# Turning the attention probabilities on VectorE in 32x32 blocks in the third stage of a decoder kernel

## The reference

```python
qkv = x @ Wqkv                       # x: 64 x 128, 16 heads of 64
q, k = rotary(l2norm(q) * qs), rotary(l2norm(k) * ksc)
sim = q @ k.T * 8                    # per head, 64 x 64
mask = (i < j) | (i > j + 32)        # causal, and at most 32 tokens back
attn = softmax(where(mask, -inf, sim))
y = y + concat_heads(attn @ v) @ Wo
y = y + (a * gelu(gate)) @ W2 + b2   # a, gate = split(layernorm(shift(y)) @ W1 + b1)
```

## Time and profile before

| what | value |
|---|---|
| time, median of 3 runs | 3386.17 us (3384.32 to 3388.98) |
| span of the profiled execution | 3389.4 us |
| PE busy in the span | 3317.7 us (98%) |
| DVE, ACT, POOL busy | 2767.5 (82%), 2803.2 (83%), 2483.0 us (73%) |
| share of PE in the chain that ended last | 95% |
| the third stage | about 565 us to the end |

### The profile page before, as it was taken

How to read it: one execution, slowest core, us unless ns; L and a number is a source line. 1 busy time by engine, 2 the same in 40 slices (tenths; PEclk the granted TensorE clock), 3 DMA queues, 4 the chain that set the end, 5 groups by cost and what they waited for, 6 DMA issues and landing times.

```text
span 3389.4 us, 120739 instructions
## 1 busy us (share of the span) xinstructions
PE 3317.7 (98%) x49605; PEld 2474.5 (73%) x49605; DVE 2767.5 (82%) x5297; ACT 2803.2 (83%) x5522; POOL 2483.0 (73%) x4812
## 2 busy tenths in 40 slices
PE   8989998999999999999999999999999999999997
PEld 6777876577777777777777777777777777777776
DVE  6844445888888888888888888888888888899995
ACT  5756665688888888888888888888888888888885
POOL 4622223888888888888888888888888888888884
PEclk8999999999999999999999999999999999999999
DMA  3000001544444444445444444444444444444441
GB/s 108 3 7 9 8 9 35 102 83 84 85 91 98 94 84 82 83 94 105 88 82 83 89 94 98 85 86 83 95 102 83 85 85 92 83 89 85 89 88 41
DMA packets 200381, 260.15 MB, mean 77 GB/s; under 512 B 123161, under 2 KB 145438, under 8 KB 199838
## 3 DMA queue, kind: packets, MB, share of 16 engines
q0 software_dynamic: 55296, 201.35, 31.4%
q1 hardware_dynamic: 143820, 50.88, 6.1%
q10 hardware_dynamic: 722, 0.21, 0.0%
HBM read 23.95 MB, written 2.10 MB: 8 GB/s over the span
## 4 chain that ended last, share of the span: by engine, by line
PE 95%; DVE 2%; POOL 1%; issue 1%; DMA 1%; ACT 1%; SPq 0%; DVEq 0%; POOLq 0%
PE bank L1059 19%; PE bank L1034 17%; PE bank L1110 10%; PE bank L1187 10%; PE bank L1158 8%; PE bank L1174 6%; PE bank L1129 5%; PE bank L1051 4%; PE bank L675 2%; PE bank L1124 2%; PE bank L688 2%; PE bank L697 2%; PE bank L752 2%; PE bank L367 1%; PE bank L660 1%; PE bank L377 1%
## 5 line engine op out<-in xcount | busy, mean ns | idle before, releaser
L1348 DVE TENSOR_TENSOR R<-bank,tables 128x1024 f32<-128x1024 f32 x768 | 904.7, 1220 | 174.7 <-ACT sq L1246 167.2
L1059 PE MATMUL bank<-WA,xcT 128*128 128x512 f32 x1536 | 723.6, 593 | 3.0 <-ACT xcT L1221 2.1
L1034 PEld LDWEIGHTS bank<-ident,R 128*128 128x128 f32 x3072 | 365.0, 141 | 214.7 <-issue 201.2
L1361 DVE TENSOR_REDUCE ss<-sq 128x16 f32<-128x1024 f32 x384 | 460.1, 1198 | 0.0
L1473 POOL TENSOR_TENSOR P<-P,inv_sum 128x512 f32<-128x512 f32 x384 | 447.6, 1331 | 2.9 <-DVE inv_sum L1402 2.9
L1246 ACT ACTIVATE sq<-bank 128x512 f32<-128x512 f32 x768 | 431.3, 587 | 16.0 <-PE bank L1059 16.0
L1034 PE MATMUL bank<-ident,R 128*128 128x128 f32 x3072 | 431.2, 273 | 8.8 <-POOL R L1461 6.8
L1461 POOL TENSOR_TENSOR R<-R,rn 128x512 f32<-128x512 f32 x384 | 400.4, 1043 | 31.5 <-DMA R<-R 5.4
L1467 POOL TENSOR_TENSOR P<-P,rn 128x512 f32<-128x512 f32 x384 | 402.6, 1048 | 4.3 <-DVE P L1390 4.3
L1059 PEld LDWEIGHTS bank<-WA,xcT 128*128 128x128 f32 x1536 | 262.2, 191 | 188.9 <-issue 184.0
L1187 PE MATMUL bank<-WO,OT 128*128 128x128 f32 x3072 | 374.6, 275 | 0.0
(11 more groups left out here) (154 smaller groups left out, 6857.6 us busy)
## 6 DMA issues: line engine op xcount, KB each, us to landing
R<-R POOLq DMA_DIRECT2D x384, 512.0 KB, 5.0
WA<-in_wqkv SPq DMA_DIRECT2D x24, 256.0 KB, 2.9
ystat<-Y SPq DMA_DIRECT2D x192, 32.0 KB
ystat<-Y SPq DMA_DIRECT2D x384, 15.8 KB
ys<-Y SPq DMA_DIRECT2D x192, 32.0 KB
ys<-Y SPq DMA_DIRECT2D x384, 15.8 KB
WV<-in_wqkv SPq DMA_DIRECT2D x6, 512.0 KB, 4.0
WO<-in_wo SPq DMA_DIRECT2D x6, 512.0 KB, 4.3
```

What stands on the lines that cost most here:

```text
L1034: return nc.tensor.transpose(dst, src, m.ident[:, :])
L1059: mm(b[QK_BANK[n, half]][:, :], m.xsT[:, t % 2, :], cols[:, half, :, :], start=True, stop=True)\
L1348: tt(both, src.unsqueeze(1).to_broadcast([128, 2, 16, 32]), tab.unsqueeze(2).to_broadcast([128, 2, 16, 32]), ALU.mult).then_inc(s.rotated. ...
L1361: nc.vector.tensor_reduce(m.ss[:, t % 2, 16 * n:16 * n + 16], m.sq[:, n, :].rearrange("p (h d) -> p h d", d=HD), AX.X, ALU.add)\
```

## The change

In the third stage, TensorE no longer turns the probabilities and ScalarE no longer copies them out of PSUM. Instead:

- VectorE turns each half of a tile's P (128x512) with one instruction of 32x32 blocks, into a new buffer Z (two tiles of it). Z has three slots of 256 columns for each head parity; the blocks of keys 0 to 31 go to slot 1, those of keys 32 to 63 to slot 2. These two instructions stand between `squares_summed(i, KEYS)` and `ff_added(i-8)`, and the first also waits until TensorE has read Z for the tile before last.
- A block turned in place lies in the partitions of its queries. SyncE therefore moves two blocks for each sequence with DMAs (four a tile, each 32 partitions by two runs of 1 KB): slot 1 of the first 32 partitions to slot 0, and slot 1 of the second 32 to slot 2 of the first 32. What the masked block leaves is zero; slot 0 of the second 32 partitions is zeroed once by GpSimd, in front of its cross-attention loop. The four DMAs stand at the end of SyncE's pass, behind `weights(i)`, and wait for VectorE.
- `head_outputs` reads Z in slots 0 and 2 (a moving operand of 2 x 32 columns), 32 products of 64x64 as before, and waits for the DMAs.
- `values` makes two products of full width (128 rows by 512 columns), where there were four with 64 output rows each, so V lies by token and not by sequence. The copies into V stay two of 512 columns.
- The copies of the head outputs (OT) write in another column order, and `out_projection` reads eight adjacent pieces.
- Waits follow: `input_turned` on `o_copied` in place of `p_copied`, `queries(t, 1)` on `v_copied`; `less_maximum` no longer waits for TensorE's turning.

The core of the diff:

```diff
+        m.Z = sb("Z", [128, 2, 2, 3, 256])
...
+        pool.memset(m.Z[:, :, :, :, :], 0.0)
         for i in range(N + 2):
             probs_scaled(i - 1, 1)
...
+        def probs_moved(t):
+            if exists(t):
+                sp.wait_ge(s.p_turned.sem, s.p_turned.upto(0, t + 1))
+                z, done = m.Z[:, t % 2, :, :, :], s.p_moved[t % 2]
+                for bb in range(2):
+                    first, second = slice(64 * bb, 64 * bb + 32), slice(64 * bb + 32, 64 * bb + 64)
+                    sp.dma_start(z[first, :, 0, :], z[first, :, 1, :]).then_inc(done, 16)
+                    sp.dma_start(z[first, :, 2, :], z[second, :, 1, :]).then_inc(done, 16)
...
             if i < N:
                 weights(i)
+            probs_moved(i - 3)
...
-                for e in range(2):
-                    last = mm(V_BANK[bb][64 * e:64 * e + 64, :], m.xsT[:, t % 2, bb * 64:bb * 64 + 64],
-                              cols[:, e, :, :], start=True, stop=True)
-                last.then_inc(s.v.sem, 1)
+                mm(V_BANK[j][:, :], m.xsT[:, t % 2, :], m.WV[:, j * 512:(j + 1) * 512], start=True, stop=True)\
+                    .then_inc(s.v.sem, 1)
...
-        def probs_turned(t, j):
-            if exists(t):
-                pe.wait_ge(s.normal.sem, s.normal.upto(j, t + 1))
...
-                for n in range(4):
-                    at = j * 512 + n * 128
-                    last = turned(PT_BANK[j][:, n * 128:(n + 1) * 128], m.P[:, t % 2, at:at + 128])
-                last.then_inc(s.p_turned.sem, 1)
...
+                for hp in range(PAIRS):
+                    for bb, a in ((0, 0), (1, 1), (0, 1), (1, 0)):
+                        rows, head, vals = slice(64 * bb, 64 * bb + 64), slice(64 * a, 64 * a + 64), (2 * hp + a) * 64
+                        probs = m.Z[rows, t % 2, a, 0:3:2, hp * 32:hp * 32 + 32]
+                        last = mm(PV_BANK[bb][head, hp * 64:hp * 64 + 64], m.V[rows, t % 4, vals:vals + 64], probs,
+                                  start=True, stop=True)
...
-        def probs_out(t, j):
-            if exists(t):
-                act.wait_ge(s.p_turned.sem, s.p_turned.upto(j, t + 1))
-                copy(m.PT[:, t % 2, j * 512:(j + 1) * 512], PT_BANK[j][:, :]).then_inc(s.p_copied.sem, 1)
...
+        def probs_turned(t, a):
+            if exists(t):
+                dve.wait_ge(s.normal.sem, s.normal.upto(a, t + 1))
+                if a == 1:
+                    at_least(dve, s.o, 2 * (t - 1))
+                blocks = m.P[:, t % 2, a * 512:(a + 1) * 512].rearrange("p (h k n) -> p k h n", k=2, n=32)
+                nc.vector.transpose(m.Z[:, t % 2, a, 1:3, :].rearrange("p k (h n) -> p k h n", n=32), blocks)\
+                    .then_inc(s.p_turned.sem, 1)
...
             squares_summed(i, KEYS)
+            probs_turned(i - 3, 1)
+            probs_turned(i - 3, 0)
             ff_added(i - 8)
```

More of the change, by code:

```diff
@@ L1066, in queries @@
                     pe.wait_ge(m.w_in, 64 * layer(t) + 64)
+                else:
+                    at_least(pe, s.v_copied.sem, s.v_copied.upto(1, t))
                 heads_in(t, QUERIES, half)
@@ L1097, in queries_turned, with values @@
                 last.then_inc(s.q_turned.sem, 1)
-        def values(t, bb):
+        def values(t, j):
             if exists(t):
-                cols = m.WV[:, :].rearrange("p (j e n) -> p e j n", e=2, n=128)
-                if bb == 1:
+                if j == 1:
                     pe.wait_ge(m.w_v, 16 * layer(t) + 16)
@@ L1132, in scores @@
                             last.then_inc(s.scores, 1)
-        def probs_turned(t, j):
-            if exists(t):
-                pe.wait_ge(s.normal.sem, s.normal.upto(j, t + 1))
-                if j == 0:
-                    at_least(pe, s.o_copied.sem, s.o_copied.upto(1, t))
-                else:
-                    pe.wait_ge(s.v_copied.sem, s.v_copied.upto(1, min(t + 4, N)))
-                    if t >= N - 3:
-                        pe.wait_ge(s.xn_copied, t - 2)
-                for n in range(4):
-                    at = j * 512 + n * 128
-                    last = turned(PT_BANK[j][:, n * 128:(n + 1) * 128], m.P[:, t % 2, at:at + 128])
-                last.then_inc(s.p_turned.sem, 1)
         def ff_in(t):
@@ L1163, in head_outputs @@
             if exists(t):
-                pe.wait_ge(s.p_copied.sem, s.p_copied.upto(0, t + 1))
+                pe.wait_ge(s.p_moved[t % 2], 64 * (t // 2) + 64)
                 pe.wait_ge(s.v_copied.sem, s.v_copied.upto(0, t + 1))
@@ L1168, in head_outputs @@
                     pe.wait_ge(s.rotated.sem, s.rotated.upto((QUERIES, 0), t + 5))
-                for j in range(4):
-                    for bb in range(2):
-                        for e, a in ((0, 0), (1, 1), (0, 1), (1, 0)):
-                            keys, head = slice(64 * e, 64 * e + 64), slice(64 * a, 64 * a + 64)
-                            vals, probs = bb * 512 + j * 128 + a * 64, (4 * a + j) * 128 + bb * 64
-                            last = mm(PV_BANK[e][head, j * 128 + bb * 64:j * 128 + bb * 64 + 64],
-                                      m.V[keys, t % 4, vals:vals + 64], m.PT[keys, t % 2, probs:probs + 64],
-                                      start=True, stop=True)
-                            if j == 3 and bb == 1 and (e, a) in ((0, 1), (1, 0)):
-                                last.then_inc(s.o, 1)
+                for hp in range(PAIRS):
[4 more added lines that the diff above has]
+                                  start=True, stop=True)
+                        if hp == PAIRS - 1 and (bb, a) in ((0, 1), (1, 0)):
+                            last.then_inc(s.o, 1)
         def out_projection(t):
@@ L1185, in out_projection @@
                 for c in range(PAIRS):
-                    at = (c % 2) * 512 + c // 2 * 128
-                    last = mm(OUT[:, 0:128], m.OT[:, t % 2, at:at + 128], wo[:, c * 128:(c + 1) * 128],
+                    last = mm(OUT[:, 0:128], m.OT[:, t % 2, c * 128:c * 128 + 128], wo[:, c * 128:(c + 1) * 128],
                               start=(c == 0), stop=(c == PAIRS - 1))
@@ L1230, in outputs_out @@
                 act.wait_ge(s.o, 2 * t + 2)
-                copy(m.OT[:, t % 2, e * 512:(e + 1) * 512], PV_BANK[e][:, :]).then_inc(s.o_copied.sem, 1)
+                copy(m.OT[:, t % 2, :].rearrange("p (c b q) -> p b c q", b=2, q=SEQ)[:, e, :, :],
+                     PV_BANK[e][:, :].rearrange("p (c q) -> p c q", q=SEQ)).then_inc(s.o_copied.sem, 1)
         def normal_out(t):
```

12 lines of the change are left out of this document (3 added, 9 removed).

## The result

| | before | after |
|---|---|---|
| median of the runs | 3387.43 us (3384.32 to 3388.98) | 3599.82 us (3596.59 to 3608.22) |
| profiled span | 3389.4 us | 3601.1 us |
| one pass of the third stage, median | 14.45 us | 15.46 us |

The changed kernel takes 1.0633 times as long, 95% interval 1.0617 to 1.0649. The forecast was 3576 us, 5.6% slower; it came out 6.3% slower, inside the range of 3465 to 3680 us.

The account below looks back on a forecast made before the run. TensorE, busy 98% of the span, was taken as the bound; afterwards a round through ff_added of 15.48 us replaces 14.45. 184 passes add 190 us: span 3579, time 3576 us, 5.6% slower, range 3465 to 3680.

Parts of the forecast that it names:

- The round through `ff_added`: From ff_in over TensorE, ScalarE and VectorE's ff_added back to ff_in: 15.48 us a pass after the change.
- The turnings: Two new VectorE instructions of 128x512 float32 in front of ff_added: 0.60 us each, 1.20 us a pass.
- The quick and the slow rival: VectorE's turnings at 0.32 us each, 3472 us, chance 0.07; or at 1.14 us each, 3774 us, chance 0.07.
- The gain on TensorE: Turnings of P and part of the values leave TensorE: 1.08 us a pass, all becoming idle time.
- the values: TensorE's products into V, two full ones for eight half-width instructions: 1.72 us instead of 1.87, 0.15 less.
- 3.9 us against 2.02 of issues: SyncE's queue behind the moves: time left for ys before the statistics need them, against their three issues; no wait counted.
- The rival for late ys: ys reach the statistics 1 us late through SyncE's queue or DMA: 0.64 us a pass, about 3694 us; chance 0.07.
- step 4: The two new turnings on VectorE, in front of ff_added, as part of the round: 1.20 us.
- the rival *Faster: VectorE's work bounds the pass at 13.98 us, 3300 us; needs turnings under 0.17 us together on the round; chance 0.04.
- The clock: TensorE's granted clock falls to its lower level in the longer wait: 2.3 us a pass, near 4000 us; chance 0.03.
- The prediction's own sign of being wrong: In the third stage, a granted clock below 1.00 would show the forecast wrong.
- What would show it: Third stage: passes of about 15.5 us, ff_in waiting 1.8 to 2.1 us for VectorE, turnings near 0.68 us.

Follow-up runs that it names:

- experiment 1: The kernel before with two VectorE turnings of a 128x512 buffer nobody reads, in front of ff_added in each pass: 3571.67 us, ratio 1.0542.
- experiment 5: The changed kernel with SyncE's DMAs of ystat issued one pass earlier, in front of the moves, all moves kept: 3571.4 us, ratio 1.0547.
- experiment 4: The changed kernel without the four DMAs a tile, head_outputs waiting for VectorE's turnings instead: 3569.82 us, ratio 1.0542.
- experiment 3: The changed kernel without VectorE's two turnings of P, waits and moves kept, Z left at zeros: 3395.22 us, ratio 1.0028.
- experiments 8 to 12: The changed kernel reordered, turnings ending VectorE's pass, values moved ahead; variants move ff_added, drop moves or split values: 3613.48, 3638.25, 3526.94, 3588.9, 3532.78 us.

## Why the prediction was right, and where it was off

**The mechanism: right, and shown.** The round through `ff_added`, not the amount of work, sets the pass. Experiment 1 puts only the two turnings into the kernel before and gets 15.46 us a pass; experiment 2 moves them by half a pass and gets 14.56. (The 184 passes are 184 x 14.45 = 2659 us, 78% of the span of before and not almost all of it.)

**The turnings: right.** Forecast 0.60 us of pitch each; the row has 686 ns for one, and 2125.77 - 2124.55 = 1.22 us for the two. The quick and the slow rival are out. By the rule of two elements a cycle, weighed in the prediction from the Trainium skill's "VectorE: DVE Perf Modes", section "What auto-detection actually checks", each would have taken near 0.32 us by the prediction's estimate; the trace doesn't bear it out. The one element per cycle of the Trainium skill's "Vector Engine (DVE) Microarchitecture Reference", section 3.8, fits the trace: 0.61 us for 512 elements, where the rotation takes 0.55 for 512 more.

**The gain on TensorE: right that it turns into idle time.** Its size was 0.98 us a pass by the waits of experiment 1, against 1.08. One term was mis-sized, the values: they take 2123.08 - 2121.16 = 1.92 us from start to start, where 1.72 was forecast and the kernel before has 1.87, so the gain of 0.15 us didn't come. (From start to start that leaves 0.93 - 0.05 = 0.88; the 0.1 us to the 0.98 of the waits stays open.) It costs nothing, behind it TensorE waits anyway. `head_outputs` with its 2 x 32 columns takes 1.09 us from start to start, 2121.16 - 2120.07. In the kernel before it takes the same, 2034.52 - 2033.43:

```profile
2033.43 1.16 PE L1174 MATMUL bank<-PT,V 64*64 64x64 f32 x64
2034.52 0.65 PE L1110 MATMUL bank<-WV,xcT 128*64 128x512 f32 x2
```

**What was off: the cover for ys.** The term that was mis-sized is "3.9 us against 2.02 of issues", taken at nothing in the sum. I had found the queue free 1 us after `attention_added`; in the pass shown it was 2131.77 - 2129.96 = 1.81 us. From the event to the statistics it takes 1.81 + 2.03 of issues + 1.17 to land = 5.0 us, where I had counted the issues and not the landing. (The 3.9 us can't be worked out from the rows shown either: 4.31 less 1 is 3.3. In the pass shown VectorE was ready 4.77 us after the event, which less 1 would be 3.8.) I had also taken each issue at its usual length, while single ones take 0.6 to 1.2 us more, and had left out the loads of weights. The cost is 28 us by experiment 5 and 30 by experiment 4, in 27 long passes; the sum 184 x 1.01 = 186 plus about 29 is 215, and the span grew by 211.7. The rival for late ys named this mechanism, but at 0.64 us in every pass, 118 us: late ys lengthen 17 passes of 183, and the fall of the clock ten more. The forecast's error of 24 us is about these 28 less 4 for a round forecast 0.02 us too long.

**A round that I had not walked.** "Without step 4 it is 14.28" is true of that round, but experiment 3 shows another of 14.45 us through ScalarE's second copy of V. It did not touch the forecast, since 15.48 is above both. It does touch the rival *Faster*: its point of decision, turnings of less than 0.17 us in all, would have brought nothing.

**The clock: put at nothing too, and it came in ten passes.** The rival named the mechanism, a fall to the lower level in TensorE's longer wait, but for every pass and at 2.3 us each, 420 us. Measured are ten passes of 183, each 1.4 to 2.8 us longer, 18.0 us in all, behind waits of 1.96 to 2.30 us. The waits of 1.75 us, which most passes have, never brought a fall. The prediction's own sign of being wrong, a granted clock below 1.00 in the third stage, was therefore there (0.99 from 720 to 3300 us), though too small to move the forecast out of its range.

**What would show it.** As forecast were the wait of `ff_in`, the turnings' length, and no more wait of the row sums for the exponents. VectorE's idle time before the queries' rotation was 0.86 in one pass and 1.18 in the other (forecast 0.9); 0.87 is the usual value. The 0.36 us before the keys' rotation is there in experiments 1 and 4, and gone in the pass shown, where the queries' rotation had started late.

## What to carry to other kernels

Where one engine is busy for all of the time and another hands it something 0.4 us before it is needed, walk the round between them and ask where on it a new instruction stands: the same two took 186 us in front of the hand-over and 20 us half a pass later. Walk every round that comes back to the same wait, because the second was 0.17 us above the first. In a DMA queue shared by several steps, count for each step when it could be issued, what stands before it at its longest, its own issues, its landing, and the loads that come only in some passes. Look at the granted clock pass by pass: a mean of 0.99 hid ten passes that cost more than the delays in front of them. And where an engine stands still and waits for nobody, look whether a packet of the instruction queue ended just before it goes on.

## What the runs showed of the hardware that I had not expected

- TensorE stood still inside a run of products with no wait in it 52 to 59 times in about 180 passes in each of the kernels of experiments 8 to 12: 1.6 to 2.3 us on average, at most 4.4, 82 to 130 us in all in the scores. Each time it went on 1.17 to 1.71 us after a 16 KB packet of the instruction queue had ended, always at the start of a block of 256 of its records. Why the packets begin late stays open.
- TensorE's granted clock fell to 0.50 in ten passes of the changed kernel, each time around the end of a wait of 1.96 to 2.30 us (seven other waits of 1.91 us or more brought none); 161 waits of 1.83 us or less brought no fall. Such a pass was 1.4 to 2.8 us longer.
- A turning of 128x512 elements of 4 bytes in 32x32 blocks took VectorE 686 ns and 0.61 us from start to start, from a strided source (P) and in experiments 1 and 2 from an adjacent one (E, 1.29 and 1.25 us for two) alike.
- One and the same DMA issue on SyncE held its queue for 0.54 us in one pass and 1.29 in the next, right behind the four moves both times.
- A move between partitions of 64 KB landed 2.5 us after its issue began (median); the last ys landed, by VectorE's start, 1.15 to 1.17 us after its issue ended.
